# Feed-forward norm variances: tokens turned on TensorE with VectorE batch statistics, in place of a centring matmul, squares and a contraction

## The chip, the cores and the metric

One core of one Trainium2 chip runs the whole program in one launch. The metric is device time in microseconds (us) of that execution; the time before is the median of three runs.

## What is computed

The input x has 8 items of 512 tokens with 128 channels. The result is x plus two branches that both start from a layer norm of x: a global attention with 16 heads, and six layers of windowed attention and feed-forward. The change touches the norm at the head of each feed-forward part:

```python
def ffn_layer(x, g, bln, W1, b1, W2, b2):
    mu = x.mean(-1, keepdims=True)
    var = ((x - mu) ** 2).mean(-1, keepdims=True)
    xn = (x - mu) / jnp.sqrt(var + 1e-05) * g + bln
    hg = xn @ W1 + b1
    a, gate = jnp.split(hg, 2, -1)
    return a * jax.nn.gelu(gate, approximate=False) @ W2 + b2
...
for i in range(DEPTH):   # 6
    x = attn_layer(shift_tokens(x), Wqkv[i], q_scale[i], k_scale[i], Wo[i]) + x
    x = ffn_layer(shift_tokens(x), ln_g[i], ln_b[i], W1[i], b1[i], W2[i], b2[i]) + x
```

Everything is fp32. g, bln and the subtraction of the mean are folded into W1 ahead of the layers, so a layer needs only 1/sqrt(var + 1e-5) for each token at run time.

## The kernel before

The program has two parts, one after the other. The first (`global_attention_part`) computes the global attention and prepares weights; it opens with a layer norm on VectorE by batch statistics (L461, L465), the only such instructions before the change. The second (`layers_part`) takes about six sevenths of the span, and the change lies wholly in it.

**Items and bodies.** Six layers times eight batch items make 48 work items. Activations lie with channels on the 128 partitions and the 512 tokens along the free side; a token's channels are therefore spread over partitions, and 128 tokens make one block (T = 4 blocks). The order of work is written out by hand: each engine has a `body` that is run for i from -1 to 53 and in which stage k works on item i - k. The stages of one item on TensorE: in the body where it is x_1, its 16 projections (`project`, L970, 980) and the sums of their squares (`square_sums`, L982, 990); as x_2, the norms spread to keys (`spread_norms`, L1014, 1018), the scores (L1029) and two sets of token transposes (L1038); as x_3, `attend` (L1041, 1049); as x_4, the output projection (`combine`, L1054, 1061), `centred` (L1065) and `variance` (L1000); as x_5, `spread_rstd` (L1007), the up projections (L1078) and `down` (L1080, 1085). All engines thus work on different items in one body, and one body is one period of the steady stage. The first bodies fill this pipeline and the last ones drain it.

**The variances before.** When x_4's feed-forward input xf is there (L1346 on ScalarE), TensorE multiplies it by a centring matrix (`centred`, between projections 12 and 13), ScalarE squares the result into csq (`centred_squares`, L1352), and at the end of the body TensorE contracts each of the four 128-token blocks of csq with a column of 1/128 (`variance`, L1004). The four columns of variances lie behind the 128 columns of query and key norm sums in the tile sq_sums. VectorE's `norms` (L1168) then runs one chain of eleven dependent instructions over all 132 columns (L1178, and `rsqrt`, L56 to 65): it yields the norms of item x_1 and the reciprocal deviation of item x_4 together.

**What orders the work.** Engines meet through semaphores only, and each engine's queue is in order. The tile pair_ps is a ring of two PSUM slots that most of TensorE's results share. `slot` (L952) gives the next one and first makes TensorE wait until the user two places back has been read out. In a full body the order of ring users is: keys 0, keys 1, rstd, scores 0, u 0 to 3 (two for each `attend`), scores 1, up 0, u 4, u 5, keys 2, up 1, keys 3, the centred result, u 6, u 7, up 2, scores 2, scores 3, token transposes. So u 6 takes the slot of keys 3, and u 7 the slot of the centred result; `attend` takes both slots before its first matmul. Keys 0 takes the slot of scores 3, which is free when VectorE's `mask_scores` has read it.

VectorE's order in the part around the change is products 10 and 11, `gated` 1, `scale_keys` 3, products 12 and 13, `prob_blocks` 0, `gated` 2, products 14, `mask_scores` 2 with its maxima and sums, `ffn_sum`, products 15, `norms`, `prob_blocks` 1, `mask_scores` 3.

Of the kernel before, what the change touches and what calls it, by code (L numbers as in the profile page):

```python
# [20 lines left out]
P = 128  # L21
B, N, C = 8, 512, 128
T = N // P
# [709 lines left out]
NSUM = T * 2 * LH  # L733
NRN = NSUM + T
STEPS = 1 + RSQRT_LINKS
LATE = 3
# [3 lines left out]
def layers_part(nc, X, d):  # L740
# [10 lines left out]
    with ExitStack() as ctx:  # L751
# [11 lines left out]
        b2 = few[:, LAYERS * TILES:LAYERS * (TILES + 1)]  # L763
        mean = few[:, NFEW - 2:NFEW - 1]
        magic = few[:, NFEW - 1:NFEW].bitcast(I32)

        tables = sb("tables", [P, 4, N])
        ident = sb("ident", [P, P])
        centre = sb("centre", [P, P])
        heads = sb("heads", [P, UNITS, 2, 32])  # L770
# [20 lines left out]
        xf = sb("xf", [P, N])  # L791
        csq = sb("csq", [P, N])
        xn = sb("xn", [P, N])
# [44 lines left out]
        xf_done = tally("xf_done", 2)  # L838
        xc_ready = tally("xc_ready", 1)
        csq_done = tally("csq_done", 1)  # L840
        var_ready = tally("var_ready", 1)
        rb_ready = tally("rb_ready", 1)
# [23 lines left out]
        def _(sp):  # L866
# [15 lines left out]
            for g in range(1, UNITS):  # L882
                load_wqk(0, g)
            for dst, src in ((mask, d["mask"]), (eps, d["eps"]), (centre, d["centre"])):
                sp.dma_start(dst[:], src).then_inc(consts, 16)
# [63 lines left out]
        def _(pe):  # L949
            ring = {"used": 0, "freed": [None, None], "to": None}  # L950

            def slot(name, freed_by, value):  # L952

                k = ring["used"] % 2
                if ring["freed"][k] is not None:
                    last, count = ring["freed"][k]
                    pe.wait_ge(last.sem, count)
                ring["freed"][k] = (freed_by, value)
                ring["used"] += 1
                where[name] = k  # L960
                return k
# [20 lines left out]
            def square_sums(n, g):  # L982
                if g == 0 and n:
                    pe.wait_ge(steps.sem, steps.at(n - 1, STEPS))
                elif g == 0:
                    pe.wait_ge(consts, 16 * 5)
                for side in range(2):
                    pe.wait_ge(sq_added.sem, sq_added.at(n, 2 * g + side + 1))
                    for t in range(T):
                        last = pe.matmul(nq_ps[32 * t:32 * t + 32, 0:P], heads[:, g, side, :], sq[:, 2 * side, t * P:(t + 1) * P],  # L990
                                         start=(g == 0 and side == 0), stop=(g == UNITS - 1 and side == 1), skip_group_check=True)
                last.then_inc(ns_ready.sem, 1)
# [6 lines left out]

            def variance(n):  # L1000
                pe.wait_ge(csq_done.sem, csq_done.at(n, 1))
                pe.wait_ge(steps.sem, steps.at(n + LATE - 1, STEPS))
                for t in range(T):
                    last = pe.matmul(sq_sums[:, P + t:P + t + 1], csq[:, t * P:(t + 1) * P], mean, start=True, stop=True, skip_group_check=True)  # L1004
                last.then_inc(var_ready.sem, 1)

            def spread_rstd(n):  # L1007
                pe.wait_ge(steps.sem, steps.at(n + LATE, STEPS))
                k = slot(("rstd", n), xn_done, xn_done.at(n, 1))
                for t in range(T):  # L1010
                    last = pe.transpose(pair_ps[:, k, 0, t * P:(t + 1) * P], rn[:, (n + LATE) % 2, NSUM + t:NSUM + t + 1].to_broadcast([P, P]), ident[:])
                last.then_inc(rb_ready.sem, 1)
# [51 lines left out]

            def centred(n):  # L1065
                pe.wait_ge(xf_done.sem, xf_done.at(n, 2))
                k = slot(("xc", n), csq_done, csq_done.at(n, 1))
                pe.matmul(pair_ps[:, k, 0, :], centre[:], xf[:], start=True, stop=True).then_inc(xc_ready.sem, 1)

# [30 lines left out]
            def body(i, x_ahead, x_0, x_1, x_2, x_3, x_4, x_5, x_6):  # L1100
# [31 lines left out]
                if x_1 is not None: square_sums(x_1, 2); project(x_1, 12)  # L1132
                if x_4 is not None: centred(x_4)
                if x_1 is not None: project(x_1, 13)
# [9 lines left out]
                if x_1 is not None: sums_by_token(x_1)  # L1144
                if x_4 is not None: variance(x_4)
                if x_3 is not None: combine(x_3, 0, 1)
# [6 lines left out]
        def _(dve):  # L1153
# [14 lines left out]
            def norms(k):  # L1168
                if not 0 <= k < ITEMS + LATE:
                    return  # L1170
                lo, hi = (0 if k < ITEMS else NSUM), (NRN if k >= LATE else NSUM)
                if k == 0:
                    dve.wait_ge(consts, 16 * 5)
                if k < ITEMS:
                    dve.wait_ge(ss_ready.sem, ss_ready.at(k, 1))
                if k >= LATE:
                    dve.wait_ge(var_ready.sem, var_ready.at(k - LATE, 1))
                dve.scalar_tensor_tensor(sq_sums[:, lo:hi], sq_sums[:, lo:hi], TINY, eps[:, lo:hi], ALU.max, ALU.add).then_inc(steps.sem, 1)  # L1178
                dve.wait_ge(steps.sem, steps.at(k, 1))
                rsqrt(dve, rn[:, k % 2, lo:hi], sq_sums[:, lo:hi], rt[:, lo:hi], magic.to_broadcast([P, hi - lo]), steps, k, 1)  # L1180

            def normalise(n):
# [63 lines left out]
            def body(i, x_ahead, x_0, x_1, x_2, x_3, x_4, x_5, x_6):  # L1246
# [15 lines left out]
                if x_2 is not None: scale_keys(x_2, 3)  # L1262
                if x_1 is not None: products(x_1, 12, 13)
                if x_2 is not None: prob_blocks(x_2, 0)
# [4 lines left out]
                if x_5 is not None: ffn_sum(x_5)  # L1269
                if x_1 is not None: products(x_1, 15)  # L1270
                norms(i - 1)
                if x_2 is not None: prob_blocks(x_2, 1); mask_scores(x_2, 3)
# [14 lines left out]
        def _(act):  # L1287
# [59 lines left out]

            def centred_squares(n):
                act.wait_ge(xc_ready.sem, xc_ready.at(n, 1))
                if n:  # L1350
                    act.wait_ge(var_ready.sem, var_ready.at(n - 1, 1))
                act.activation(csq[:], pair_ps[:, where["xc", n], 0, :], ACT.Square).then_inc(csq_done.sem, 1)  # L1352

            def gates(n, c):
# [6 lines left out]
            def body(i, x_ahead, x_0, x_1, x_2, x_3, x_4, x_5, x_6):  # L1361
# [15 lines left out]
                if x_1 is not None: squares(x_1, 12)  # L1377
                if x_4 is not None: centred_squares(x_4)
                if x_1 is not None: squares(x_1, 13)
# [119 lines left out]
def constants():  # L1499
    p = np.arange(P)  # L1500
    heads = np.zeros((P, UNITS, 2, 2 * LH), np.float32)
    for g in range(UNITS):
        for side in range(2):
            heads[p, g, side, LH * side + 4 * g + p // HALF] = 1
    eps = np.zeros((P, NRN), np.float32)
    eps[:, NSUM:] = EPS
    return {
        "ident": np.eye(P, dtype=np.float32),
        "centre": (np.eye(P) - 1.0 / C).astype(np.float32),
        "heads": heads,  # L1510
        "eps": eps,
        "mask": score_mask(),
        "ga_rope": rope_tables(),
        "rot": rotation_tables(),
    }
# [54 lines left out]
```

## Time and profile before

| | |
|---|---|
| median of 3 runs | 3474.66 us (3468.48 to 3475.24) |
| the profiled execution: span | 3463.4 us; its time outside the span is not given, and the three runs lie 5 to 12 us above the span |
| mean granted TensorE clock | 0.982 |
| TensorE matmul busy | 3295.0 us, 95% |
| VectorE busy | 2841.0 us, 82% |
| ScalarE busy | 1825.1 us, 53% |
| GpSimd busy | 2637.8 us, 76% |
| DMA | mean 78 GB/s |

Busy shares are averages over the first part, the filling, the steady stage and the drain. PE is TensorE's matmuls and PEld its weight loads, which lie beside them. A matmul's record overlaps the next one's, since they are pipelined: the time that one takes from the queue is the distance to the next start, and the chain of waits shows it.

### The profile page before, as it was taken

The page shows a single profiled execution, that of the slowest core. Times are in us where ns is not written, and L with a number is a line of the kernel's source. Part 1 is how long each engine was busy: PE and PEld are TensorE (multiplying, and loading weights), DVE is VectorE, ACT ScalarE, POOL GpSimd, SP SyncE. Part 2 cuts the span into 40 slices and gives each one's busy share as a digit, 9 for nine tenths or more (in the row PEclk, how much of TensorE's full clock was granted, in tenths as well). Part 3 has the DMA queues.
Part 4 walks back from the last instruction along what each step waited for, and adds up shares of the span by engine and source line. Part 5 has one row for each costly group of instructions (what it writes and reads, how often), then busy time and mean ns, then how long its engine had stood idle before and what let it go on. Part 6 is the DMA issues. An engine that isn't in the chain of part 4 may idle for free.

```text
span 3463.4 us, 71935 instructions
## 1 busy us (share of the span) xinstructions
PE 3295.0 (95%) x27964; PEld 1634.9 (47%) x27964; DVE 2841.0 (82%) x3289; ACT 1825.1 (53%) x2684; POOL 2637.8 (76%) x1918
## 2 busy tenths in 40 slices
PE   6899976899999999999999999999999999999987
PEld 4333333454545454555545454555555454555443
DVE  6899937888888888888888888888888888888863
ACT  2578843455454555555454555555454555555442
POOL 3223228988888888888888888888888888888860
PEclk7899988999999999999999999999999999999999
DMA  6333133333333333333323333323333233333331
GB/s 211 81 61 64 37 103 78 74 74 74 81 73 83 77 72 72 85 81 75 80 68 77 76 85 78 72 70 86 81 73 79 71 77 76 86 75 74 74 75 30
DMA packets 178111, 270.05 MB, mean 78 GB/s; under 512 B 42480, under 2 KB 67056, under 8 KB 176112
## 3 DMA queue, kind: packets, MB, share of 16 engines
q1 hardware_dynamic: 174032, 251.03, 30.0%
q10 hardware_dynamic: 3744, 14.43, 1.2%
q8 instruction: 225, 3.69, 0.5%
q14 instruction: 110, 0.90, 0.1%
HBM read 44.43 MB, written 19.55 MB: 18 GB/s over the span
## 4 chain that ended last, share of the span: by engine, by line
PE 65%; DVE 5%; POOL 5%; SPq 4%; ACT 4%; issue 1%; DMA 1%; POOLq 0%; DVEq 0%; ACTq 0%
PE ly_to_ps L1061 19%; PE ly_pj_ps L980 14%; PE ly_pair_ps L1029 8%; PE ly_pair_ps L1049 7%; SPq L906 4%; PE ly_pair_ps L1078 4%; PE ly_to_ps L1085 4%; DVE ly_prod L1165 3%; ACT ly_u L1339 3%; PE ly_pair_ps L1018 2%; PE ly_nq_ps L990 2%; DMA ly_kbd<-ly_kr 1%; PE ly_pair_ps L1038 1%; POOL ly_kr L1412 1%; POOL ly_kr L1411 1%
## 5 line engine op out<-in xcount | busy, mean ns | idle before, releaser
L1165 DVE SCALAR_TENSOR_TENSOR ly_prod<-ly_pj_ps,ly_few,ly_tables 128x1024 f32<-128x1024 f32 x768 | 964.6, 1272 | 189.7 <-ACT ly_sq L1308 171.6
L1308 ACT ACTIVATE ly_sq<-ly_pj_ps 128x512 f32<-128x512 f32 x768 | 451.1, 602 | 745.6 <-PE ly_pj_ps L980 701.9
L980 PE MATMUL ly_pj_ps<-ly_xs,ly_wqk 128*128 128x512 f32 x1536 | 795.1, 615 | 34.2 <-DVE ly_prod L1165 21.8
L1061 PE MATMUL ly_to_ps<-ly_u,ly_mvo 128*128 128x512 f32 x1536 | 720.6, 598 | 0.2 <-DVE x_all L1238 0.2
L1417 POOL TENSOR_TENSOR ly_sq<-ly_sq 128x512 f32<-128x512 f32 x384 | 490.7, 1278 | 229.1 <-ACT ly_sq L1308 228.7
L1339 ACT COPY ly_u<-ly_pair_ps 128x1024 f32<-128x1024 f32 x384 | 378.7, 1013 | 239.0 <-PE ly_pair_ps L1049 239.0
L1421 POOL TENSOR_TENSOR ly_sx<-ly_sx,ly_smax 128x1024 f32<-128x1024 f32 x192 | 365.4, 1903 | 145.1 <-DVE ly_smax L1205 145.1
L980 PEld LDWEIGHTS ly_pj_ps<-ly_xs,ly_wqk 128*128 128x128 f32 x1536 | 268.8, 191 | 426.2 <-issue 291.5
L1061 PEld LDWEIGHTS ly_to_ps<-ly_u,ly_mvo 128*128 128x128 f32 x1536 | 277.1, 190 | 287.2 <-issue 287.2
L1049 PE MATMUL ly_pair_ps<-ly_pt,ly_xt 32*128 32x512 f32 x3072 | 383.9, 613 | 20.0 <-ACT ly_u L1339 13.0
L1029 PE MATMUL ly_pair_ps<-ly_kbd,ly_qp 128*32 128x128 f32 x12288 | 376.0, 276 | 24.2 <-DMA ly_kbd<-ly_kr 21.0
L1029 PEld LDWEIGHTS ly_pair_ps<-ly_kbd,ly_qp 128*32 128x32 f32 x12288 | 330.8, 111 | 142.8 <-issue 98.9
L1433 POOL TENSOR_TENSOR ly_sx<-ly_sx,ly_rsum 128x1024 f32<-128x1024 f32 x192 | 365.3, 1903 | 24.3 <-DVE ly_rsum L1213 24.3
L1428 POOL TENSOR_TENSOR ly_sx<-ly_sx,ly_rn 128x1024 f32<-128x1024 f32 x192 | 365.4, 1903 | 7.0
L497 DVE TENSOR_REDUCE ga_mx<-ga_f_ps 128x2 f32<-128x1024 f32 x256 | 299.5, 1220 | 32.0 <-PE ga_f_ps L331 31.6
L648 ACT ACTIVATE ga_pt<-ga_s_ps 128x512 f32<-128x512 f32 x512 | 277.7, 597 | 73.7 <-PE ga_s_ps L354 59.9
L1078 PE MATMUL ly_pair_ps<-ly_xn,ly_w1c 128*128 128x512 f32 x576 | 275.8, 601 | 4.7 <-ACT ly_u L1339 4.6
L1325 ACT ACTIVATE ly_sx<-ly_sx 128x1024 f32<-128x1024 f32 x192 | 203.3, 1059 | 120.7 <-POOL ly_sx L1428 120.2
L1191 DVE TENSOR_TENSOR ly_kr<-ly_kr,ly_pair_ps 128x1024 f32<-128x1024 f32 x192 | 232.9, 1213 | 32.5 <-PE ly_pair_ps L1018 32.4
L1198 DVE TENSOR_TENSOR ly_sx<-ly_pair_ps,ly_mask 128x1024 f32<-128x1024 f32 x192 | 232.9, 1213 | 24.7 <-PE ly_pair_ps L1029 14.9
L1049 PEld LDWEIGHTS ly_pair_ps<-ly_pt,ly_xt 32*128 32x128 f32 x3072 | 143.8, 184 | 224.7 <-issue 166.8
L1411 POOL TENSOR_TENSOR ly_kr<-ly_prod 128x512 f32<-128x512 f32 x192 | 244.6, 1274 | 4.2 <-DMA ly_kbd<-ly_kr 3.8
(122 smaller groups left out, 4351.8 us busy)
## 6 DMA issues: line engine op xcount, KB each, us to landing
ly_qp<-ly_qr SPq DMA_DIRECT2D x768, 128.0 KB, 2.3
ly_kbd<-ly_kr SPq DMA_DIRECT2D x1536, 64.0 KB, 2.0
ga_parts_dram<-ga_parts SPq DMA_DIRECT2D x16, 384.0 KB, 2.5
ga_qs<-ga_parts_dram SPq DMA_DIRECT2D x96, 64.0 KB
ga_ks<-ga_parts_dram SPq DMA_DIRECT2D x96, 64.0 KB
ly_wqk<-in_wqk SPq DMA_DIRECT2D x24, 256.0 KB, 3.4
ly_mvo<-mvo_dram SPq DMA_DIRECT2D x6, 1024.0 KB, 6.5
mvo_dram<-ga_pt ACTq DMA_DIRECT2D x4, 1024.0 KB, 6.1
```

Source lines behind the costliest of these rows:

```text
L980: pe.matmul(pj_ps[:, j % 2, :], wqk[:, g, j % TILES, :], xs[:, n % 2, WIN:], start=True, stop=True).then_inc(proj_ready.sem, 1)
L1029: last = pe.matmul(pair_ps[32 * c:32 * c + 32, k, t // 2, at:at + 128], qp[:, g, p, WIN * w:WIN * w + WIN], kbd[:, g % 2, p, :, WIN * w:WI ...
L1049: mm = pe.matmul(pair_ps[:, ks[c // 2], c % 2, :], xt[rows, late, t, :], pt[rows, t, :, late, :], start=(late == 0), stop=(late == 1), ski ...
L1061: last = pe.matmul(to_ps[:], mvo[:, h, :], u[:, :, :, h, :].rearrange("p t c q -> p (t c) q"), start=(h == 0), stop=(h == LH - 1))
L1078: pe.matmul(pair_ps[:, k, side, :], w1c[:, at:at + P], xn[:], start=True, stop=True).then_inc(h_ready.sem, 1)
L1165: dve.scalar_tensor_tensor(prod[:, k], pj_ps[:, j % 2, :].unsqueeze(1).to_broadcast([P, 2, N]), gains[:, n // B, k:k + 1], tables[:, table ...
L1308: act.activation(sq[:, k, :], pj_ps[:, j % 2, :], ACT.Square).then_inc(sq_done.sem, 1)
L1339: act.copy(u[:, k // 2, at:at + 2].rearrange("p c h q -> p c (h q)"), pair_ps[:, where["u", n, k]]).then_inc(u_copied.sem, 1)
L1417: pool.tensor_tensor(sq[:, 2 * (k % 2)], sq[:, 2 * (k % 2)], sq[:, 2 * (k % 2) + 1], ALU.add).then_inc(sq_added.sem, 1)
L1421: pool.tensor_tensor(sx[:, g % 2], sx[:, g % 2], smax[:, g % 2].unsqueeze(3).to_broadcast([P, T, 4, SPAN]), ALU.subtract).then_inc(s_less. ...
L1428: pool.tensor_tensor(sx[:, g % 2], sx[:, g % 2], rq.unsqueeze(3).to_broadcast([P, T, 4, SPAN]), ALU.mult).then_inc(s_scaled.sem, 1)
L1433: pool.tensor_tensor(sx[:, g % 2], sx[:, g % 2], rsum[:, g % 2].unsqueeze(3).to_broadcast([P, T, 4, SPAN]), ALU.mult).then_inc(p_ready.sem, 1)
```

## The change

- On TensorE, `centred` is replaced by `turn_ffn_tokens` at the same place: four 128x128 transposes of xf into one ring slot, so that each token's channels lie along the free side. Its slot is freed by VectorE (`halves_done`) where it was freed by ScalarE. `variance` is taken out.
- On VectorE, `token_halves` (four batch-statistics instructions, from PSUM) stands between products 12 and 13, and `variances` (four aggregations, which write mean and variance of each block's tokens) stands just ahead of `norms`. The waits for the earlier steps and for the summed norms that `variance` had or implied move with it.
- On ScalarE, `centred_squares` is taken out.
- The chain of `norms` runs over 136 columns, since each block now has a mean beside its variance.
- The centring matrix is not loaded in the second part any more, and the waits for constants count one less.

```diff
-NRN = NSUM + T
+NRN = NSUM + 2 * T
...
-            def variance(n):
-                pe.wait_ge(csq_done.sem, csq_done.at(n, 1))
-                pe.wait_ge(steps.sem, steps.at(n + LATE - 1, STEPS))
-                for t in range(T):
-                    last = pe.matmul(sq_sums[:, P + t:P + t + 1], csq[:, t * P:(t + 1) * P], mean, start=True, stop=True, skip_group_check=True)
-                last.then_inc(var_ready.sem, 1)
...
-                    last = pe.transpose(pair_ps[:, k, 0, t * P:(t + 1) * P], rn[:, (n + LATE) % 2, NSUM + t:NSUM + t + 1].to_broadcast([P, P]), ident[:])
+                    last = pe.transpose(pair_ps[:, k, 0, t * P:(t + 1) * P], rn[:, (n + LATE) % 2, NSUM + 2 * t + 1:NSUM + 2 * t + 2].to_broadcast([P, P]), ident[:])
...
-            def centred(n):
+            def turn_ffn_tokens(n):
                 pe.wait_ge(xf_done.sem, xf_done.at(n, 2))
-                k = slot(("xc", n), csq_done, csq_done.at(n, 1))
-                pe.matmul(pair_ps[:, k, 0, :], centre[:], xf[:], start=True, stop=True).then_inc(xc_ready.sem, 1)
+                k = slot(("turned", n), halves_done, halves_done.at(n, 1))
+                for t in range(T):
+                    last = pe.transpose(pair_ps[:, k, 0, t * P:(t + 1) * P], xf[:, t * P:(t + 1) * P], ident[:])
+                last.then_inc(xt_turned.sem, 1)
...
-                if x_4 is not None: centred(x_4)
+                if x_4 is not None: turn_ffn_tokens(x_4)
...
-                if x_4 is not None: variance(x_4)
...
                 if k >= LATE:
-                    dve.wait_ge(var_ready.sem, var_ready.at(k - LATE, 1))
+                    dve.wait_ge(var_done.sem, var_done.at(k - LATE, 1))
...
+            def token_halves(n):
+                dve.wait_ge(xt_turned.sem, xt_turned.at(n, 1))
+                if n:
+                    dve.wait_ge(var_done.sem, var_done.at(n - 1, 1))
+                k = where["turned", n]
+                for t in range(T):
+                    last = dve.bn_stats(halves[:, t, :], pair_ps[:, k, 0, t * P:(t + 1) * P])
+                last.then_inc(halves_done.sem, 1)
+
+            def variances(n):
+                dve.wait_ge(halves_done.sem, halves_done.at(n, 1))
+                dve.wait_ge(steps.sem, steps.at(n + LATE - 1, STEPS))
+                if n + LATE < ITEMS:
+                    dve.wait_ge(ss_ready.sem, ss_ready.at(n + LATE, 1))
+                for t in range(T):
+                    last = dve.bn_aggr(sq_sums[:, NSUM + 2 * t:NSUM + 2 * t + 2], halves[:, t, :])
+                last.then_inc(var_done.sem, 1)
...
-                if x_1 is not None: products(x_1, 12, 13)
+                if x_1 is not None: products(x_1, 12)
+                if x_4 is not None: token_halves(x_4)
+                if x_1 is not None: products(x_1, 13)
...
+                if x_4 is not None: variances(x_4)
                 norms(i - 1)
...
-            def centred_squares(n):
-                act.wait_ge(xc_ready.sem, xc_ready.at(n, 1))
-                if n:
-                    act.wait_ge(var_ready.sem, var_ready.at(n - 1, 1))
-                act.activation(csq[:], pair_ps[:, where["xc", n], 0, :], ACT.Square).then_inc(csq_done.sem, 1)
...
-                if x_4 is not None: centred_squares(x_4)
```

## Rows read from the trace of the kernel before

**Rows 1.** The page, part 1: busy time of each engine.
```profile
PE 3295.0 (95%) x27964; PEld 1634.9 (47%) x27964; DVE 2841.0 (82%) x3289; ACT 1825.1 (53%) x2684; POOL 2637.8 (76%) x1918
```

**Rows 2.** Busy time by stretch, with granted clock, DMA share and GB/s last.
```profile
585.00:645.00 60.00, 49.75 (x465) 26.80 (x465) 50.95 (x57) 26.30 (x38) 55.87 (x39) 0.91 0.31 75
...
2004.28:2063.93 59.65, 59.25 (x509) 30.47 (x507) 50.99 (x58) 31.55 (x44) 52.21 (x37) 1.00 0.36 90
...
3320.00:3380.00 60.00, 48.37 (x429) 26.43 (x428) 36.49 (x55) 23.23 (x27) 30.46 (x18) 1.00 0.31 80
```

**Rows 3.** Waits of PE in 900 to 3330 us: us in total, times, longest.
```profile
PE ly_pair_ps L1049 <- ACT ly_u L1339: 7.7, 40, 0.2
PE ly_pj_ps L980 <- DVE ly_prod L1165: 6.9, 41, 0.2
PE ly_pair_ps L1029 <- DMA ly_kbd<-ly_kr: 3.3, 8, 0.9
```

**Rows 4.** Chain of waits, one body: start, us of the chain, what.
```profile
2046.76 0.44 PE ly_pair_ps L1018 x4
...
2048.82 0.97 PE ly_pair_ps L1068 x2
...
2064.04 0.79 PE ly_nq_ps L1004 x8
```

**Rows 5.** Instructions on tile ly_xf: centring matmuls, min/median/max ns, first and last start.
```profile
L1068 PE MATMUL ly_pair_ps<-ly_xf,ly_centre x96: 592/592/668, 673.8 to 3437.3; 128*128 128x512 f32 x96
```

**Rows 6.** Timeline of PE, one body: start, us, engine, line.
```profile
2011.99 1.04 PE L1018 MATMUL ly_pair_ps<-ly_ident,ly_rnx 128*128 128x128 f32 x8
...
2048.70 1.10 PE L1068 MATMUL ly_pair_ps<-ly_xf,ly_centre 128*128 128x512 f32 x2
...
2050.59 2.00 PE L1049 MATMUL ly_pair_ps<-ly_pt,ly_xt 32*128 32x512 f32 x16
```

**Rows 7.** Timeline of ACT, the same body: the squares of the centred result.
```profile
2049.83 0.60 ACT L1352 ACTIVATE ly_csq<-ly_pair_ps 128x512 f32<-128x512 f32 x1 [0.38 <-PE ly_pair_ps L1068]
```

**Rows 8.** Timeline of DVE, the same body, around products 12 and 13.
```profile
2044.29 1.22 DVE L1191 TENSOR_TENSOR ly_kr<-ly_kr,ly_pair_ps 128x1024 f32<-128x1024 f32 x1 [0.62 <-PE ly_pair_ps L1018]
...
2049.60 1.28 DVE L1165 SCALAR_TENSOR_TENSOR ly_prod<-ly_pj_ps,ly_few,ly_tables 128x1024 f32<-128x1024 f32 x1
2051.32 1.28 DVE L1165 SCALAR_TENSOR_TENSOR ly_prod<-ly_pj_ps,ly_few,ly_tables 128x1024 f32<-128x1024 f32 x1 [0.43 <-ACT ly_sq L1308]
...
2056.35 0.75 DVE L1231 SCALAR_TENSOR_TENSOR ly_hid<-ly_pair_ps,ly_w1c,ly_hid 128x512 f32<-128x512 f32 x1 [2.36 <-ACT ly_hid L1359]
```

**Rows 9.** Timeline of DVE, the start of that body: products 15, norms, mask_scores 3.
```profile
2004.12 1.28 DVE L1165 SCALAR_TENSOR_TENSOR ly_prod<-ly_pj_ps,ly_few,ly_tables 128x1024 f32<-128x1024 f32 x1
2005.31 0.29 DVE L1178 SCALAR_TENSOR_TENSOR ly_nq_ps<-ly_nq_ps,ly_eps 128x132 f32<-128x132 f32 x1
...
2010.32 1.23 DVE L1198 TENSOR_TENSOR ly_sx<-ly_pair_ps,ly_mask 128x1024 f32<-128x1024 f32 x1
```

**Rows 10.** Timeline of DVE in the first part: batch statistics, and one small step.
```profile
3.63 0.88 DVE L461 BATCH_NORM_STATS2 ga_stats<-ga_xt 128x6 f32<-128x128 f32 x4 [0.40 <-DMA ga_xt<-in_x]
4.54 0.38 DVE L465 BATCH_NORM_AGGREGATE ga_mv<-ga_stats 128x2 f32<-128x6 f32 x4
...
6.04 0.16 DVE L58 SCALAR_TENSOR_TENSOR ga_rstd<-ga_var,ga_magic 128x4 int32<-128x4 int32 x1
```

**Rows 11.** Timeline of the drain: mask_scores 3, key spreading, squares, attend, small step.
```profile
3326.47 1.22 DVE L1198 TENSOR_TENSOR ly_sx<-ly_pair_ps,ly_mask 128x1024 f32<-128x1024 f32 x1
...
3327.84 1.06 PE L1018 MATMUL ly_pair_ps<-ly_ident,ly_rnx 128*128 128x128 f32 x8 [1.25 <-DVE ly_sx L1198]
...
3360.94 0.60 ACT L1352 ACTIVATE ly_csq<-ly_pair_ps 128x512 f32<-128x512 f32 x1 [2.20 <-PE ly_pair_ps L1068]
3361.68 2.00 PE L1049 MATMUL ly_pair_ps<-ly_pt,ly_xt 32*128 32x512 f32 x16 [0.78 <-ACT ly_csq L1352]
...
3377.05 0.16 DVE L58 SCALAR_TENSOR_TENSOR ly_rn<-ly_nq_ps,ly_few 128x4 int32<-128x4 int32 x1
```

More of the change, by code:

```diff
@@ L763, in layers_part @@
         b2 = few[:, LAYERS * TILES:LAYERS * (TILES + 1)]
-        mean = few[:, NFEW - 2:NFEW - 1]
         magic = few[:, NFEW - 1:NFEW].bitcast(I32)
@@ L768, in layers_part @@
         ident = sb("ident", [P, P])
-        centre = sb("centre", [P, P])
         heads = sb("heads", [P, UNITS, 2, 32])
@@ L791, in layers_part @@
         xf = sb("xf", [P, N])
-        csq = sb("csq", [P, N])
+        halves = sb("halves", [P, T, 6])
         xn = sb("xn", [P, N])
@@ L838, in layers_part @@
         xf_done = tally("xf_done", 2)
-        xc_ready = tally("xc_ready", 1)
-        csq_done = tally("csq_done", 1)
-        var_ready = tally("var_ready", 1)
+        xt_turned = tally("xt_turned", 1)
+        halves_done = tally("halves_done", 1)
+        var_done = tally("var_done", 1)
         rb_ready = tally("rb_ready", 1)
@@ L883, in _ @@
                 load_wqk(0, g)
-            for dst, src in ((mask, d["mask"]), (eps, d["eps"]), (centre, d["centre"])):
+            for dst, src in ((mask, d["mask"]), (eps, d["eps"])):
                 sp.dma_start(dst[:], src).then_inc(consts, 16)
@@ L985, in square_sums @@
                 elif g == 0:
-                    pe.wait_ge(consts, 16 * 5)
+                    pe.wait_ge(consts, 16 * 4)
                 for side in range(2):
@@ L1172, in norms @@
                 if k == 0:
-                    dve.wait_ge(consts, 16 * 5)
+                    dve.wait_ge(consts, 16 * 4)
                 if k < ITEMS:
@@ L1505, in constants @@
     eps = np.zeros((P, NRN), np.float32)
-    eps[:, NSUM:] = EPS
+    eps[:, NSUM + 1::2] = EPS
     return {
```

## The prediction

> **What bounds the kernel now.** I read the page first: TensorE has 95% busy, VectorE 82%, ScalarE 53% [rows 1]. That is an average over stages, so the busy times of one steady body come next: a body takes 59.65 us, in which TensorE is busy 59.25 and VectorE 50.99 [rows 2]. TensorE's waits in the steady stage come to 18 us in about 41 bodies, under 0.5 each, half of it just behind its own results [rows 3]. So TensorE bounds a body by the length of its queue, and what is taken out of that queue is worth its full time, but only as far as nothing else arrives later than TensorE then does. The 8.7 us in which VectorE is idle do not say that. What says it is the time of each hand-over between the two, so I read one body in the timelines of both engines.
>
> **What TensorE gives up.** In the chain, the centring matmul (two records) takes 0.97 us and the contraction's eight records 0.79 [rows 4]. Four 128x128 transposes take 0.44, as the spreading of keys does with the same shape [rows 4]. Net 0.97 + 0.79 - 0.44 = 1.32 us a body. There are 48 of them (96 records of centring, two each [rows 5]). ScalarE gives up one 0.60 us square a body [rows 7] at 53% busy; only `attend` 3 waits for it, which is treated next. The load of the centring matrix and the shorter wait for constants lie before the first body, among loads that no row shows TensorE waiting for: nothing.
>
> **Hand-over A: the ring slot of the turned tokens.** `attend` 3 takes the slots of keys 3 and of the centred result. Now the squares free the latter: they end at 2049.83 + 0.60 = 2050.43 [rows 7]. In the drain, `attend` starts 0.14 after such a square (3361.54 to 3361.68 [rows 11]), which gives 2050.57; the row says 2050.59 [rows 6]. So this read-out is already just as late as TensorE. After the change VectorE frees the slot, and its four statistics instructions stand behind product 12. That one starts at 2049.60 [rows 8], and the next instruction can start 1.19 after such a start (2004.12 to 2005.31 [rows 9]): 2050.79. The transposed tokens are there by then, since TensorE reaches that place at 2048.70 [rows 6]. Four statistics of 128 columns take 0.88 from first start to last end [rows 10]: 2051.67, and with 0.14 `attend` starts at 2051.81. That is 1.22 us later than today, although TensorE itself would be there 0.5 earlier. Can VectorE be earlier? From 2044.29 on it works without a gap up to product 12, and what it waited for at 2044.29 is TensorE's key spreading in the same body [rows 8]; so the whole piece moves with TensorE, and 1.22 is not made up. Product 13 slips by about 0.3, `prob_blocks` 0 with `attend`, and both have the 2.36 us idle ahead of `gated` 2 [rows 8]; everything from there to `down` follows `attend` through ScalarE and moves by the same 1.22.
>
> Those rows of statistics read SBUF, the new ones PSUM. One and the same small step takes 0.16 us from SBUF [rows 10] and 0.16 from PSUM [rows 11], so I keep 0.88. Bounds: above, four times the 0.29 of a 132-column step on PSUM [rows 9], 1.16; below, the columns alone: (0.29 - 0.16)/128 a column [rows 9, 11], four times 128 of them, 0.52. It cannot be nothing, as VectorE's queue is in order. A is then +0.86 to +1.50. The Trainium skill ("VectorE: DVE Perf Modes", section "The TRN2 errata") gives a VectorE instruction 120 cycles of fixed cost from PSUM against 58 from SBUF at 0.96 GHz, by which the four would take 0.26 us more (an estimate from that page) and A would be +1.48; the two 0.16 us rows do not agree with it, and I go by them.
>
> **Hand-over B: the norms chain.** TensorE loses the 0.79 of the contraction right after `down`, so it comes earlier to its next wait on VectorE: the key spreading in the next body, whose slot `mask_scores` 3 frees. That ends at 2010.32 + 1.23 = 2011.55 [rows 9]. In the drain the spreading starts 0.15 after that instruction ends (3327.69 to 3327.84 [rows 11]), so it could start at 2011.70 and does at 2011.99 [rows 6]: 0.29 of slack. The change puts onto VectorE ahead of it: four aggregations, 0.38, and the hand-over to the chain, 0.03 (4.51 to 4.54) [rows 10]; and four more columns in eleven steps, 11 x 4 x 0.001 = 0.05. Together 0.46, so the release comes at 2012.16 while TensorE is ready at 2011.99 - 0.79 = 2011.20. It waits, and the 0.79 is gone with 0.17 more. Bounds: the aggregations at least 0.16 (one small step), at most four such steps, 0.64 [rows 11]; B is 0 to +0.43. `variances` itself waits for nothing that comes late: its statistics are 13 us old, the summed norms come from TensorE before product 15 ends. Queued behind it are `norms`, the widening on ScalarE, GpSimd's scaling of scores; these start later by 0.46 in a stretch where TensorE is later by 0.17, and their own slack has to take 0.3 us.
>
> **The sum.** A body gets 1.22 + 0.17 = 1.39 us longer instead of 1.32 shorter. Bodies 4 to 48 have both this item and projections, 45 of them: +63. Two small terms go the other way: the 3.3 us in which scores waited for the keys' copies [rows 3] vanish, as `attend` gives those copies 1.2 us more; and in the three bodies of the drain VectorE has little to do, so they save about 1 us each. Sum +56 us: the profiled span of 3463.4 would be about 3519. The median is 11 us above that span and gets the same: 3474.7 + 56 = 3531. With both bounds, 45 x 0.86 - 6 = +32 and 45 x 1.93 - 6 = +81: 3507 to 3556.
>
> **The rivals.**
> - Further ties (0.13). With VectorE 0.3 later against TensorE in the first half of a body, other waits could bind: the slot of the reciprocal deviations behind the scaled keys, projection 6 behind product 4, scores 0 behind the keys' copies. If one costs up to 0.5 us a body, 45 x 0.5 = 22 on top of the forecast or its upper bound: 3553 to 3578. For it: DMA already delays scores in 8 bodies [rows 3]. Against: those delays are 0.4 us on average.
> - Only A binds (0.08). If the key spreading did not wait for `mask_scores` 3, TensorE would keep the 0.79: 45 x (1.22 - 0.79) - 6 = +13, 3488. Against: the drain's row names that very releaser [rows 11].
> - Faster (0.08). The turned tokens' slot does not decide: VectorE gets to the statistics before TensorE has passed projection 13, because the longer waits elsewhere let it run ahead. It decides if VectorE's product 12 ends by 2049.6, not 2050.88 [rows 8], 1.3 us before its row; with B hidden too, 48 x 1.32 = 63 us fall away: 3411. For it: 8.7 us idle a body. Against: none of that idle time lies between 2044.29 and product 12.
> - The new read-out ends up as early as the squares did and B eats the rest: no change, 3475 (0.04).
> - The clock falls (0.02). TensorE would idle 2 us at a stretch twice a body. If its granted clock went to the 0.91 of the filling stage [rows 2], part of the time at 1.2 in place of 2.4 GHz, a body of 60 us would lose 5.4 of work: +240, 3770. Against: with only 48.4 of 60 us busy the drain has 1.00 [rows 2]. The Trainium skill ("TensorE: Matmul & The Clock Gate", "Part 4: PE-mode transpose") says that transposes do not keep the clock up as matmuls do, which speaks for this rival; the steady body, full of the same transposes, has 1.00 [rows 2], and four more of them do not look like enough.
>
> **How the numbers follow.** The forecast has 0.65. Under 0.2% (7 us) a measurement of this kernel can't tell a change from none. Slower: 0.65 + 0.13 + 0.08 + 0.02 = 0.88; same 0.04; faster 0.08. The range 3488 to 3572 takes in the bounds, most of the ties and half of the case in which only A binds: about 0.8.
>
> **What the profile after would show.** A steady body of about 61.0 us; `attend` at line 1049 waiting some 1.5 us a body for VectorE's statistics, which it now hardly does for any but its own read-outs; the key spreading at line 1018 waiting about 1 us for `mask_scores`; four statistics in 0.9 us and four aggregations in 0.4; the clock still 1.00; the copies' waits gone. If the body is under 59.5 us, A is wrong: either the statistics start earlier or the slot is not the one I count. If it is over 62, a wait that I have at nothing has come up.

## The result, and the profile after

| | before | after |
|---|---|---|
| median | 3471.57 us (4 runs) | 3529.67 us (4 runs, 3528.55 to 3531.09) |
| ratio to before | | 1.0169 (95% interval 1.0153 to 1.0186) |
| profiled span | 3463.4 us | 3528.6 us |
| mean granted clock | 0.982 | 0.981 |

The kernel became slower by 58 us; the forecast was 3531 against a median before of 3474.7, that is +56. Part 1 of the page after, which answers to [rows 1]:

```profile
PE 3251.7 (92%) x27676; PEld 1591.3 (45%) x27676; DVE 2893.8 (82%) x3673; ACT 1795.5 (51%) x2636; POOL 2640.0 (75%) x1918
```

TensorE is busy for 43 us less and ScalarE for 30 us less; VectorE has 53 us more. None of these differences is by itself the 65 us by which the profiled span grew. The waits of PE in 900 to 3390 us of the changed kernel (line of the waiting matmul, releaser, us in total, times, longest) answer to [rows 3]:

```profile
PE ly_pair_ps L1040 <- DVE ly_halves L1180: 67.5, 41, 1.7
PE ly_pair_ps L1009 <- DVE ly_sx L1208: 31.0, 40, 0.8
PE ly_pair_ps L1040 <- ACT ly_u L1352: 7.6, 40, 0.2
PE ly_pj_ps L978 <- DVE ly_prod L1157: 6.9, 41, 0.2
```

Two waits are new, 1.65 us a body at `attend` and 0.78 at the key spreading, and the waits for the keys' copies are gone. Line 1040 is `attend` (1049 before), 1009 the key spreading (1018 before), 1180 and 1189 the statistics and the aggregations, 1208 `mask_scores`.

**Hand-over A.** First PE, then DVE of one body of the changed kernel, to hold against [rows 6, 8]:

```profile
2015.09 0.63 PE L1009 MATMUL ly_pair_ps<-ly_ident,ly_rnx 128*128 128x128 f32 x4
...
2020.23 0.63 PE L1060 MATMUL ly_pair_ps<-ly_ident,ly_xf 128*128 128x128 f32 x4
2020.70 1.02 PE L978 MATMUL ly_pj_ps<-ly_xs,ly_wqk 128*128 128x512 f32 x2
2023.38 2.00 PE L1040 MATMUL ly_pair_ps<-ly_pt,ly_xt 32*128 32x512 f32 x16 [1.66 <-DVE ly_halves L1180]
```

```profile
2021.15 1.28 DVE L1157 SCALAR_TENSOR_TENSOR ly_prod<-ly_pj_ps,ly_few,ly_tables 128x1024 f32<-128x1024 f32 x1
2022.36 0.88 DVE L1180 BATCH_NORM_STATS2 ly_halves<-ly_pair_ps 128x6 f32<-128x128 f32 x4
```

The transposes are done at 2020.86, the statistics start at 2022.36, 1.21 after product 12, end at 2023.24, and `attend` starts 0.14 later. From the spreading of keys 2 to `attend` 3 it is 2023.38 - 2015.09 = 8.29 us. Before, the same spreading starts here:

```profile
2043.55 0.63 PE L1018 MATMUL ly_pair_ps<-ly_ident,ly_rnx 128*128 128x128 f32 x4
```

and 2050.59 - 2043.55 = 7.04 [rows 6]. So A costs +1.25 us.

**Hand-over B.** The timeline of DVE from `ffn_sum` on, and the PE row that waits for it; [rows 9] and the first of [rows 6] are its counterparts:

```profile
2036.56 1.27 DVE L1157 SCALAR_TENSOR_TENSOR ly_prod<-ly_pj_ps,ly_few,ly_tables 128x1024 f32<-128x1024 f32 x1
2037.75 0.37 DVE L1189 BATCH_NORM_AGGREGATE ly_nq_ps<-ly_halves 128x2 f32<-128x6 f32 x4
2038.23 0.31 DVE L1170 SCALAR_TENSOR_TENSOR ly_nq_ps<-ly_nq_ps,ly_eps 128x136 f32<-128x136 f32 x1
...
2043.30 1.22 DVE L1208 TENSOR_TENSOR ly_sx<-ly_pair_ps,ly_mask 128x1024 f32<-128x1024 f32 x1
```

```profile
2044.67 1.06 PE L1009 MATMUL ly_pair_ps<-ly_ident,ly_rnx 128*128 128x128 f32 x8 [0.78 <-DVE ly_sx L1208]
```

From product 15 to `mask_scores` 3 it was 2010.32 - 2004.12 = 6.20 us and is now 6.74. The spreading starts 0.15 after `mask_scores` ends (2044.52 to 2044.67). From `attend` 3 to the next spreading it is 21.29 us; before, the next body's row gives 21.05:

```profile
2071.64 1.04 PE L1018 MATMUL ly_pair_ps<-ly_ident,ly_rnx 128*128 128x128 f32 x8
```

So B costs +0.24, and what TensorE no longer spends on the contraction is in the wait. A body after, from the windows view (length; busy us of PE, its weight loads, DVE, ACT, POOL; granted clock, DMA share, GB/s), and one body as the distance between two transposes of the summed norms (line 996 of PE):

```profile
2044.67:2105.90 61.23, 58.40 (x499) 29.57 (x500) 52.10 (x66) 30.91 (x44) 52.37 (x37) 1.00 0.36 87
```

```profile
813.56 0.27 PE L996 MATMUL ly_nq_ps<-ly_ident,ly_nsum 128*128 128x128 f32 x1
874.70 0.27 PE L996 MATMUL ly_nq_ps<-ly_ident,ly_nsum 128*128 128x128 f32 x1
```

Most bodies have 61.15 us against 59.65 [rows 2]; the one with 61.23 has a short delay of scores 0 besides. The granted clock of this body is 1.00.

### The profile page after: what moved, and what is told of

Same layout as the page of the kernel before. It is cut to its first block, busy times and chain, and to the rows that moved or that the text cites. A ratio compares the mean times of both kernels' runs of the same rounds, so it can differ in the third digit from the quotient of the medians.

```text
span 3528.6 us, 71694 instructions
## 1 busy us (share of the span) xinstructions
PE 3251.7 (92%) x27676; PEld 1591.3 (45%) x27676; DVE 2893.8 (82%) x3673; ACT 1795.5 (51%) x2636; POOL 2640.0 (75%) x1918
## 4 chain that ended last, share of the span: by engine, by line
PE 51%; DVE 17%; POOL 7%; issue 5%; ACT 4%; SPq 1%; DMA 0%; DVEq 0%; POOLq 0%; ACTq 0%
PE ly_to_ps L1052 12%; PE ly_pj_ps L978 10%; PE ly_pair_ps L1040 8%; PE ly_pair_ps L1020 8%; PE ly_pair_ps L1071 5%; DVE ly_prod L1157 4%; PE ly_to_ps L1078 4%; ACT ly_u L1352 3%; PE ly_pair_ps L1009 3%; DVE ly_sx L1208 2%; DVE ly_pt L1229 2%; POOL ly_qr L1417 2%; POOL ly_kr L1417 2%; POOL ly_kr L1418 2%; POOL ly_qr L1418 2%
## 5 line engine op out<-in xcount | busy, mean ns | idle before, releaser
L1229 DVE STREAM_TRANSPOSE ly_pt<-ly_sx 128x1024 f32<-128x1024 f32 x192 | 233.1, 1232 | 56.5 <-PE ly_pair_ps L1040 52.9
```

## The experiments

The theory under test: the time is set by two hand-overs from VectorE to TensorE, and what a VectorE instruction costs depends on whether it stands in front of one. The main rival: VectorE's queue is longer by some 1.3 us a body, and that is what one pays. Below, "body" is the distance between two key spreadings in the steady stage.

**e1: the statistics without the hand-over.** Before, plus four statistics on xf between products 12 and 13, result unused; nothing is left out.

```diff
-                if x_1 is not None: products(x_1, 12, 13)
+                if x_1 is not None: products(x_1, 12)
+                if x_4 is not None: spare_halves(x_4)
+                if x_1 is not None: products(x_1, 13)
```

> The kernel before, with four batch-statistics instructions on xf put between products 12 and 13, whose result nobody reads; the ring slot is still freed by ScalarE's squares. Place theory (the time comes from who frees the slot that attend 3 takes): attend starts where it did, product 13 has slack, the body stays at 59.6 to 59.7 us and the ratio to before is within 1.000 to 1.002. Load theory (VectorE's queue has become longer, wherever the work stands): 0.88 us times 45 bodies, +40 us, ratio 1.011.

3470.36 us, ratio 1.0004 (0.9994 to 1.0014), body 59.64. The statistics are there (VectorE's timeline), and from keys 2 to `attend` 3 it is 2052.13 - 2045.10 = 7.03 us, as before:

```profile
2051.14 1.28 DVE L1167 SCALAR_TENSOR_TENSOR ly_prod<-ly_pj_ps,ly_few,ly_tables 128x1024 f32<-128x1024 f32 x1
2052.34 0.86 DVE L1189 BATCH_NORM_STATS2 ly_halves<-ly_xf 128x6 f32<-128x128 f32 x4
```

```profile
2045.10 0.63 PE L1020 MATMUL ly_pair_ps<-ly_ident,ly_rnx 128*128 128x128 f32 x4
...
2052.13 2.00 PE L1051 MATMUL ly_pair_ps<-ly_pt,ly_xt 32*128 32x512 f32 x16
```

The statistics read SBUF here and take 0.86 us, against 0.88 from PSUM in the changed kernel. The same work at the same place costs nothing that can be measured when no slot hangs on it. The load rival is out for A.

**e2: aggregations ahead of the norms chain, alone.** Before, plus four aggregations of a constant tile, result unused.

```diff
+                if x_4 is not None: spare_variances(x_4)
                 norms(i - 1)
```

> The kernel before, with four aggregations of a constant tile into a spare SBUF tile just ahead of the norms chain; TensorE keeps its contraction. Place theory: the chain comes 0.41 us later against 0.29 us of slack at the key spreading, so TensorE waits about 0.12 us a body there: +5 us, ratio 1.0016 (body 59.75 to 59.8). Load theory: 0.38 us times 45, +17 us, ratio 1.005.

3477.34 us, ratio 1.0021 (1.0013 to 1.0030), body 59.78: +0.13 where 0.12 was expected. The slack of 0.29 us takes the first part of the 0.41, as the prediction had it; the load rival's 1.005 is outside the interval.

**e3: the contraction put back.** The changed kernel, with the eight contraction records at their old place on xf; the result is overwritten.

```diff
                 if x_1 is not None: sums_by_token(x_1)
+                if x_4 is not None: spare_contraction(x_4)
```

> The changed kernel, with TensorE's eight contraction records of 0.79 us put back at their place (on xf, their result overwritten by the aggregations). Place theory: they lie in TensorE's wait for mask_scores 3, which falls from 0.78 to about 0, so the time stays at 3530 us within 3 (body 61.2 to 61.3). Rival (TensorE's work still counts): 0.79 times 45, +36 us, 3565.

3535.45 us, ratio 1.0191 (1.0176 to 1.0205); 3529.67 without it. TensorE's wait at the key spreading falls to 0.20 us:

```profile
PE ly_pair_ps L1017 <- DVE ly_sx L1218: 7.8, 40, 0.5
```

So 0.79 us of TensorE work costs 6 us, not 36. It is twice the 3 us that I allowed. A part is the wait that I had to add: the aggregations now wait for the contraction and start 1.26 us after product 15 (2032.65 to 2033.91), 0.07 later than without, which over 45 bodies is 3 us. The rest is not explained; that it lies in the bodies is seen from the transposes of the summed norms, where 44 bodies take 2696.8 us here (683.62 to 3380.46) and 2691.5 in the changed kernel.

```profile
2032.65 1.27 DVE L1166 SCALAR_TENSOR_TENSOR ly_prod<-ly_pj_ps,ly_few,ly_tables 128x1024 f32<-128x1024 f32 x1
2033.91 0.39 DVE L1199 BATCH_NORM_AGGREGATE ly_nq_ps<-ly_halves 128x2 f32<-128x6 f32 x4
```

**e4: the statistics first.** One line moved in the changed kernel.

```diff
-                if x_1 is not None: products(x_1, 12)
                 if x_4 is not None: token_halves(x_4)
-                if x_1 is not None: products(x_1, 13)
+                if x_1 is not None: products(x_1, 12, 13)
```

> The changed kernel, with VectorE's statistics ahead of product 12 and not behind it; all else as in the change. Place theory: the slot comes free 1.2 us earlier, attend 3 waits 0.45 us and not 1.66, products 12 and 13 have slack for projections 14 and 15: body 60.0 us, 3530 - 54 = 3476 us, ratio to before 1.001. Load theory: the same instructions, so the same 3530 us.

3484.77 us, ratio 1.0051 (1.0037 to 1.0065), body 59.94. The waits of PE over the steady stage:

```profile
PE ly_pair_ps L1009 <- DVE ly_sx L1208: 33.5, 41, 2.5
PE ly_pair_ps L1040 <- DVE ly_halves L1180: 18.1, 41, 0.4
```

The same instructions in another order give 45 of the 58 us back. Not all of the 54 expected: the body is as forecast, but the waits for the keys' copies, which the later `attend` had hidden, are back (4.6 us in 11 waits), and with the delays around them the 44 bodies average 60.14 us.

**e5 and e9: the aggregations early, and what an SBUF operand costs.** Besides the order of e4, e5 aggregates into SBUF ahead of `ffn_sum`, where VectorE is idle; one step over 8 columns brings the moments into the chain. e9 is e5 with the epsilons of that step in PSUM.

```diff
+                if x_4 is not None: variances(x_4)
                 if x_5 is not None: ffn_sum(x_5)
...
-                    last = dve.bn_aggr(sq_sums[:, NSUM + 2 * t:NSUM + 2 * t + 2], halves[:, t, :])
+                    last = dve.bn_aggr(moments[:, 2 * t:2 * t + 2], halves[:, t, :])
...
+                    last = dve.scalar_tensor_tensor(sq_sums[:, NSUM:NRN], moments[:], TINY, eps[:, NSUM:NRN], ALU.max, ALU.add)   # e5
+                    last = dve.scalar_tensor_tensor(sq_sums[:, NSUM:NRN], moments[:], TINY, eps_ps, ALU.max, ALU.add)   # e9
```

> Statistics ahead of product 12 as in the run before, and the aggregations moved ahead of ffn_sum, into VectorE's idle 1.0 us there, with their result in SBUF; one step over 8 columns (0.1 to 0.16 us) takes them into the norms chain. Place theory: TensorE's wait for mask_scores 3 falls from 0.78 to about 0.4 (0.37 and the hand-over gone, one step added), body 59.94 - 0.35 = 59.6 us, 3485 - 16 = 3469 us, ratio to before 1.000. Load theory: VectorE does a little more, so 3485 or more.

3514.20 us, ratio 1.0131 (1.0116 to 1.0146), against 3469 expected: a clear miss, and in the wrong direction. The DVE timeline of e5 has the 8-column step with 1.29 us, and the GpSimd timeline shows what ends with it:

```profile
2024.51 1.29 DVE L1172 SCALAR_TENSOR_TENSOR ly_nq_ps<-ly_moments,ly_eps 128x8 f32<-128x8 f32 x1
...
2085.15 1.47 DVE L1172 SCALAR_TENSOR_TENSOR ly_nq_ps<-ly_moments,ly_eps 128x8 f32<-128x8 f32 x1
```

```profile
2023.86 1.90 POOL L1436 TENSOR_TENSOR ly_sx<-ly_sx,ly_rn 128x1024 f32<-128x1024 f32 x1
...
2084.68 1.90 POOL L1436 TENSOR_TENSOR ly_sx<-ly_sx,ly_rn 128x1024 f32<-128x1024 f32 x1
```

The step ends at 2025.80 and 2086.62, 0.04 us after GpSimd's running instruction (2025.76, 2086.58). Both inputs of the step lie in SBUF. e9 puts one of them elsewhere.

> The run with the aggregations early, whose 8-column step took 1.29 to 1.47 us; the same instruction with one of its two inputs (the epsilons) in PSUM and not in SBUF. Port theory (a VectorE instruction with both inputs in SBUF cannot start before the running GpSimd instruction ends): the step takes 0.16 us, the body falls from 60.8 to 59.7 us, 3514 - 41 = 3473 us. Rival (the step is slow by its small size, or by coming straight behind the aggregations' result): 3514.

3463.12 us, ratio 0.9984 (0.9974 to 0.9994), body 59.52. The step's minimum, median and maximum in ns, first in e5, then in e9:

```profile
L1172 DVE SCALAR_TENSOR_TENSOR ly_nq_ps<-ly_moments,ly_eps x48: 165/1464/1647, 686.0 to 3489.3; 128x8 f32<-128x8 f32 x48
```

```profile
L1177 DVE SCALAR_TENSOR_TENSOR ly_nq_ps<-ly_moments,ly_nq_ps x48: 159/160/170, 690.9 to 3446.3; 128x8 f32<-128x8 f32 x48
```

One operand's place is worth 51 us, and e9 is 10 us below the 3473 expected. TensorE's wait at the key spreading is 0.35 in e9 (0.78 in e4), the 0.4 that e5 was to show.

**e6, e7, e8: one cover.** 0.86 us of the output projection is done before the key spreading. e7 does this to the changed kernel, e8 to e4, e6 to e5.

```diff
-                if x_2 is not None: spread_norms(x_2, 0); spread_norms(x_2, 1)
                 if x_4 is not None: combine(x_4, 6)
+                if x_2 is not None: spread_norms(x_2, 0); spread_norms(x_2, 1)
```

> The changed kernel, with only that piece of the output projection (0.86 us) put before the key spreading; statistics and aggregations where the change has them. Place theory: the 0.78 of waiting for mask_scores 3 is covered in full, body 61.23 - 0.78 = 60.45 us, 3530 - 35 = 3495 us; the 1.66 at attend stays. Rival (the two waits are one: what is covered at the first comes back at the second): 3530.

> Statistics ahead of product 12, aggregations where the change has them, and the piece of the output projection before the key spreading. Place theory: body 59.94 - 0.78 = 59.16 us, 3485 - 35 = 3450 us, the same as with the aggregations early too, since the cover is longer than the wait. If moving the aggregations matters by itself, it stays above by up to 16 us.

> As the run with the aggregations early, and TensorE does one more piece of the output projection (0.86 us) before the key spreading. Place theory: the rest of the wait for mask_scores 3 (about 0.4) is covered, body 59.6 - 0.4 = 59.2 us, 3469 - 19 = 3450 us, faster than both kernels (ratio 0.995). Against it: what follows the key spreading on VectorE (the scaling of keys) may then wait, and then the time stays at 3469.

e7: 3526.58 us, ratio 1.0166 (1.0148 to 1.0184), body 61.12. e8: 3481.71, 1.0033 (1.0016 to 1.0051), 59.93. e6: 3513.06, 1.0134 (1.0117 to 1.0150). All three missed: e7 and e8 by 32 us each, and e6 did not leave e5, whose slow 8-column step it has too. For e7 the rival named beforehand (what is covered at the first wait comes back at the second) had 3530, and it is the one that came true, though the second wait is not the one at `attend`. The wait at the key spreading is gone in e7, but here is what PE has in its place, at the spreading of the deviations:

```profile
PE ly_pair_ps L1002 <- DVE ly_kr L1201: 14.5, 40, 0.4
```

That slot hangs on the scaling of keys 0, which stands on VectorE behind `mask_scores` 3. The first wait was only the first reader of a late chain. In the changed kernel the second reader is already as good as bound: the scaling ends at 2047.97 and the spreading of the deviations starts 0.17 later, against 0.14 and 0.15 where TensorE does wait for VectorE. So one cover could gain only some 0.02 us a body.

```profile
2046.76 1.21 DVE L1201 TENSOR_TENSOR ly_kr<-ly_kr,ly_pair_ps 128x1024 f32<-128x1024 f32 x1
```

```profile
2048.14 0.60 PE L1002 MATMUL ly_pair_ps<-ly_ident,ly_rn 128*128 128x128 f32 x4
```

The theory for the next three runs, called the chain theory in their forecasts, follows from this: VectorE works without a gap from `ffn_sum` to product 4, this whole stretch comes late, and whatever TensorE covers, it meets the next reader of the stretch.

**e10, e11, e12: both waits covered.** More of the output projection goes before both; e11 is the changed kernel with it, e12 e4, e10 e9.

```diff
-                if x_2 is not None: spread_norms(x_2, 0); spread_norms(x_2, 1)
                 if x_4 is not None: combine(x_4, 6)
-                if x_1 is not None: project(x_1, 2)
+                if x_2 is not None: spread_norms(x_2, 0); spread_norms(x_2, 1)
                 if x_4 is not None: combine(x_4, 7)
+                if x_1 is not None: project(x_1, 2)
+                if x_4 is not None: combine(x_4, 8)
                 if x_5 is not None: spread_rstd(x_5)
                 if i == ITEMS + 4: turn_back(2)
-                if x_4 is not None: combine(x_4, 8, 9, 10)
+                if x_4 is not None: combine(x_4, 9, 10)
```

> The changed kernel with only those covers before both waits. Chain theory: a gain of 0.1 to 0.2 us a body over the 61.12 of the run with one cover (product 4 has 0.11 us of slack left there), so 61.0 us and 3520 us. Rival (covering both waits gives the 0.78 back): 60.45, 3495 us.

> Statistics ahead of product 12, aggregations as in the change, covers before both waits. Chain theory: body 59.93 - 0.1 = 59.8 us, 3478 us. Rival: 59.94 - 0.78 = 59.2 us, 3450 us.

> The run before with the epsilons in PSUM, and more of the output projection put before both waits that follow the norms chain: the key spreading and the spreading of the deviations. Here the theory is that VectorE works without a gap from ffn_sum to product 4, and TensorE's projection 6 needs that product; it has 0.39 us of slack before the change, 0.18 of which the chain takes. So of the 0.79 us that TensorE saves only 0.2 can be kept: body 59.45 us, 3462 us, ratio 0.997. Rival (only the two waits count, and covering them gives all back): body 58.9, 3436 us, ratio 0.990.

e11: 3516.86 us, ratio 1.0150 (1.0133 to 1.0168), body 60.86. e12: 3473.99, 1.0009 (0.9997 to 1.0021), 59.70. e10: 3454.43, 0.9954 (0.9938 to 0.9970), 59.26. The chain theory is right in kind, and its gain is low by 0.1 to 0.2 us a body. The next wait is visible in PE's list of e12: `attend` 0, whose second slot `mask_scores` 0 frees, on the same gapless stretch of VectorE.

```profile
PE ly_pair_ps L1040 <- DVE ly_sx L1209: 17.4, 35, 0.8
```

e10 is faster than both kernels, by 15 us against the one before and by 75 against the changed one. It keeps the change's arithmetic, places it otherwise and adds the 8-column step. The kernel before was not run with these covers, so how much of the 15 us they would give without the change is not shown; e9, which has no covers, is 6 us below the kernel before.

## Why the prediction was right

- **Hand-over A, +1.22.** Measured +1.25: the statistics took the 0.88 us that [rows 10] gave, from PSUM too. By the Trainium skill ("VectorE: DVE Perf Modes", "The TRN2 errata") they would have been slower by 0.26, an estimate from its cycle table; the trace does not agree, with 0.88 for four. That A is a matter of the slot and not of the instructions is shown by e1 (they cost nothing elsewhere) and e4 (earlier by one product, they cost 0.44 of waiting in place of 1.66).
- **Hand-over B, +0.17.** Measured +0.24. The chain from product 15 to `mask_scores` 3 grew by 0.54 and not 0.46: between the last aggregation and the chain's first step there are 0.11 us (2038.12 to 2038.23), where I had taken 0.03 from instructions that hand over in SBUF. The price of the rest and the slack of 0.29 were right within 0.02, as e2 shows on its own.
- **TensorE's 1.32 us.** It did give up that work, and got none of it back; but the term was sized too high. By the starts in the queue, the place of the centred result took 0.93 before (2048.70 [rows 6] to 2049.63) and takes 0.47 now (2020.23 to 2020.70), and the contraction took 0.71: from the norm sums' transpose to the next matmul it was 0.93 and is 0.22. That is 1.17 us, not 1.32. TensorE stands still for 1.25 + 0.46 = 1.71 at `attend` and 0.24 + 0.71 = 0.95 at the key spreading; the waits of 1.66 and 0.78 in the list are counted from the modelled end of the matmul in front, so they are shorter. The error did not reach the sum, since both hand-overs are set by VectorE's times. e3 shows it from the other side.

```profile
2049.63 1.02 PE L980 MATMUL ly_pj_ps<-ly_xs,ly_wqk 128*128 128x512 f32 x2
...
2063.76 0.27 PE L998 MATMUL ly_nq_ps<-ly_ident,ly_nsum 128*128 128x128 f32 x1
...
2064.69 1.96 PE L1061 MATMUL ly_to_ps<-ly_u,ly_mvo 128*128 128x512 f32 x4
```

```profile
2036.56 0.27 PE L996 MATMUL ly_nq_ps<-ly_ident,ly_nsum 128*128 128x128 f32 x1
2036.78 1.96 PE L1052 MATMUL ly_to_ps<-ly_u,ly_mvo 128*128 128x512 f32 x4
```

- **The sum.** The forecast was 1.39 us a body and +56; it was 1.50 a body and +58. The profiled spans, +65, show the parts. Up to the fourth transpose of norm sums the changed kernel is 3.9 us later (686.62 and 690.51). The next 44 bodies take 2633.7 us before and 2691.5 after, +57.9: the bodies before average 59.86 us and not 59.65, 9 us in all. I put that down to the delays by the keys' copies, the only uneven wait in the list [rows 3], for which I had taken 3.3 us; after the change the average, 61.17, is within 0.02 of the usual body.

```profile
686.62 0.27 PE L998 MATMUL ly_nq_ps<-ly_ident,ly_nsum 128*128 128x128 f32 x1
...
3320.27 0.27 PE L998 MATMUL ly_nq_ps<-ly_ident,ly_nsum 128*128 128x128 f32 x1
```

```profile
690.51 0.27 PE L996 MATMUL ly_nq_ps<-ly_ident,ly_nsum 128*128 128x128 f32 x1
...
3382.05 0.27 PE L996 MATMUL ly_nq_ps<-ly_ident,ly_nsum 128*128 128x128 f32 x1
```

  The wait list had shown only the time in which the matmul itself waited, not the body that was longer around it. What follows, the drain, takes 143.1 us before and 146.6 after: +3.4, where I had taken 3 off. The contraction's time is not saved there either (the first key spreading of the drain waits 2.50 us in place of 1.25), and the granted clock of the drain was 0.96 in place of 1.00:

```profile
3320.00:3463.40 143.40, 114.02 (x667) 57.10 (x665) 65.27 (x110) 42.89 (x52) 38.02 (x22) 1.00 0.18 48
```

```profile
3382.00:3528.50 146.50, 113.31 (x639) 54.43 (x637) 68.73 (x138) 41.13 (x49) 37.82 (x22) 0.96 0.18 47
```

  The lower clock is not the change's doing alone: e1, whose steady body is that of the kernel before, has 0.96 in its drain too, and the twelve experiments lie between 0.92 and 0.99. So both hand-overs were predicted to a tenth of a microsecond, but that the total agrees within 2 us is partly luck: the small terms were off in both directions, and the medians compared come from runs of the kernel before that differ by 9 us among themselves.
- **The rivals.** The faster one needed VectorE to be at the statistics 1.3 us before its row; e4 is the nearest thing to it, and even there TensorE waits 0.44. The clock stayed at 1.00 in the steady body with waits of 1.66 and 0.78 in it; it was lower in the drain, as said above. Further ties did not add to this change, but they are real: e7 and e8 ran into the first of them (the slot of the deviations behind the scaled keys 0, named in the prediction), e12 into `mask_scores` 0, which I had not named.
- **What I had wrong in the experiments** is what the prediction had not needed: that covering a wait gives its whole length back. It gives back only the distance to the next reader of the same late chain. One cover took the most frequent body from 61.15 to 61.14 us (e7) and from 59.95 to 59.94 (e8), measured between the transposes of the summed norms; both covers together took it to 60.87 (e11) and 59.66 (e12).

What stays open: e3's 6 us are explained only by half, and why e10 to e12 gained 0.1 to 0.2 us a body more than the chain's slack says was not looked into further.

## What to carry to other kernels

A matmul taken off the busiest engine is worth its time only if the engine's next in-order waits still come in earlier; so price a change at each hand-over, from the two engines' rows around it, and not from the busy shares. When work moves to another engine, look at what that engine frees with it (here a ring slot): its place in the queue, one instruction earlier or later, was worth 45 of the 58 us here (e4). Allow more error for the total than for a single hand-over: here the drain and the delays by transfers moved it by several us. When a wait is covered, look for the next reader of the same late chain before counting the gain.

## What was not expected of the hardware

A small VectorE instruction with both inputs in SBUF did not complete before the GpSimd instruction that was running when it came: 1.29 and 1.47 us for 8 columns in the two cases shown under e5, ending 0.04 us after GpSimd's. Over all 48 it took 1.46 us in the median, 0.165 at the shortest and 1.65 at the longest, and with one input in PSUM 0.16 us (e5 and e9). The Trainium skill ("SBUF — State Buffer", "Who interferes with whom") states this: a VectorE instruction with two SBUF inputs and a GpSimd instruction that reads SBUF share a read port, and whichever starts second is blocked for the whole of the other. The runs agree. The kernel before has a sight of something like it in its first part, where a one-input instruction from SBUF to SBUF over 4 columns takes 1.05 us and ends at 6.00, GpSimd's fill at 5.99. That instruction has only one input and the fill reads nothing, so the rule for two inputs does not cover it; it is a single case, and no run tested it. It stands right behind the rows on which the prediction priced the aggregations.

```profile
4.95 1.05 DVE L468 TENSOR_SCALAR ga_var<-ga_mv 128x4 f32<-128x4 f32 x1
```

```profile
0.77 5.22 POOL L673 MEMSET ga_ks<- 128x6144 f32 x1
```

The changed kernel does not meet the two-input case there: each step of the layers' norms chain has an operand in PSUM, and in the body read above all eleven take 0.30 to 0.31 us.
